# Four graph layers on one core: the gathering engine of three row passes waits for free ring slots once for five groups instead of once for each

## The chip, the cores and the metric

The kernel runs on one core of a Trainium2 chip. Its time is the device time of one execution in microseconds (us). Before the change it is 13066.63 us, the median of three runs (13045.7 to 13079.47).

## The reference

Four graph layers, each after a layer norm and a relu, are added to a node table `x` of 12,500 rows of 128 numbers. A graph of 200,000 edges joins the rows; the edges are sorted by `dst`, and `dst` is denser at low numbers (`12500 * u**2`). What all four layers share is a sum over edges:

```
h = relu(layernorm(x)); x = x + gcn_two_convolutions(h)       # two sums over edges: passes 0 and 1
h = relu(layernorm(x)); neigh = segment_sum(h[src], dst)      # pass 2, which also sums edge_weight
h_NN = sum(h) - neigh;  x = x + normalize(h_NN) @ W.T + b
h = relu(layernorm(x)); x = x + weighted_gcn(h, edge_weight)  # pass 3
h = relu(layernorm(x)); x = x + gated_attention_layer(h, node_vec1, src, dst)   # pass 4, then a pass over stored rows
```

All sums are float32 sums to the reference's tolerance. In passes 0 to 2 each float32 row is held as three bf16 parts whose sum is the float32 value.

## The kernel before

The edges form 1563 tiles of 128 (`NT`), in the order of `dst`. The nodes form 98 windows of 128 (`NW`). An item is one pair of a tile and a window that the tile reaches; a pass works through 1664 items (`NI`), in 104 halves of 16 (`HALF`). For one item TensorE (PE) multiplies a one-hot matrix of the tile's destinations by the tile's gathered source rows and adds the product to the PSUM bank of the window.

A pass in three parts (`pass_in_parts`, passes 0, 1 and 2) is made of these workers:

- GpSimd (POOL) runs `gather_tiles`: one indirect DMA for each tile (line 436) brings 128 source rows of 768 bytes into a ring of 64 slots in SBUF. The ring is 8 groups (`RGROUPS`) of 8 tiles (`GT`), and a pass has 196 groups. From group 8 on, line 433 waits, before each group, until the group that lay in these slots is free: `freed + g - groups + 1` counts.
- SyncE (SP) runs `relay_rows`. For each group g in order it waits until group g + lead has landed and counts that up in `s_landed` (lines 444, 445); then it waits until PE has done the last item that reads group g, and counts `s_free` up by one (lines 455, 456). The lead is 4 (`LEAD`). Every fourth group SP first loads four release counts (line 454).
- ScalarE (ACT) builds the 16 one-hot matrices of a half with 16 activations (line 527) and one wide one (line 534), into two buffers; the wide one waits for PE to be done with the half before the last.
- PE, for each half, loads 16 plan words and 4 gates into registers (line 566), waits for the half's one-hots, and at each block of 8 items for landed rows and open banks (lines 570, 571). Each item is then one matmul (line 576) with register arithmetic for its bank and its slot. In pass 2 an item has a second, small matmul (line 579) with the edge weights; only this second one then signals `s_prod`.
- VectorE (DVE) empties a bank when its window is complete (line 556) and opens it for the window 8 later.

Passes 3 (`pass_with_weights`) and 4 call the same `gather_tiles` and `relay_rows`, with other tables; pass 4 has a ring of 4 groups and a lead of 2. Each pass is one block: none begins before the one before it has ended on all engines.

Of the kernel before, what the change touches and what calls it, by code (L numbers as in the profile page):

```python
# [6 lines left out]
F = 128  # L7
# [2 lines left out]
READY_STEP = 4  # L10
RGROUPS = 8
LEAD = 4
Z_RGROUPS = 4
Z_LEAD = 2
BLOCK = 8
ACC_BANKS = 8
NPARTS = 3
# [33 lines left out]
def gnn_kernel(nc, x, src, dst, edge_weight, node_vec1, L0_W1, L0_b1, L0_W2, L0_b2, L1_W, L1_b, L2_W, L2_b,  # L51
# [17 lines left out]
    TGROUPS = TILES // GT  # L69
# [25 lines left out]
    with ctx:  # L95
# [3 lines left out]
        def sem(name):  # L99
            return ctx.enter_context(nc.semaphore(name))  # L100

        def dram(name, shape, dt=f32):
            return nc.dram_tensor(name, shape, dt, kind="Internal").ap()
# [7 lines left out]
        table16 = dram("table_parts", [NPAD, NPARTS * F], bf16)  # L111
# [22 lines left out]
        ring16 = big[:, 0:RSLOTS * RW].bitcast(bf16).rearrange("p (u f) -> p u f", f=2 * RW)  # L134
# [61 lines left out]
        s_prod = sem("product_done")  # L196
# [135 lines left out]
        def one_window(ap, w):  # L332
            return windows(ap, w).rearrange("p w f -> p (w f)")
# [84 lines left out]
        s_free = sem("rows_free")  # L418

        def tiles_of(g):  # L420
            return min(GT, NT - g * GT)

        def landed_count(no, g):

            whole = sum(tiles_of(k) for k in range(g % RGROUPS, TGROUPS, RGROUPS))
            return 16 * (no * whole + sum(tiles_of(k) for k in range(g % RGROUPS, g + 1, RGROUPS)))

        def gather_tiles(pool, no, tab, slots, groups, width):

            freed = no * (TGROUPS - RGROUPS)  # L430
            for g in range(TGROUPS):
                if g >= groups:
                    pool.wait_ge(s_free, freed + g - groups + 1)
                for k in range(tiles_of(g)):
                    t = g * GT + k
                    pool.indirect_dma_start(  # L436
                        out=slots[:, t % (groups * GT), 0:width], out_offset=None, in_=tab,
                        in_offset=bass.IndirectOffsetOnAxis(ap=idx_tab[:, t // P, t % P:t % P + 1], axis=0),
                    ).then_inc(gathered[g % RGROUPS], 16)

        def relay_rows(sp, no, groups, lead, s_done, done0):

            def landed(g):
                sp.wait_ge(gathered[g % RGROUPS], landed_count(no, g))
                sp.sem_inc(s_landed[no], 1)

            for g in range(lead):
                landed(g)
            for g in range(TGROUPS):
                if g + lead < TGROUPS:  # L450
                    landed(g + lead)
                if g + groups < TGROUPS:
                    if g % 4 == 0:
                        releases = table_values(sp, RELEASE, g, 4, NI)
                    sp.wait_ge(s_done, releases[g % 4] + done0)
                    sp.sem_inc(s_free, 1)

        def table_values(eng, tab, start, n, largest):

            _, vals = nc.values_load_multi_w_load_instructions(  # L460
                tab[:, bass.ds(start, n)], engines=[eng.engine], min_val=0, max_val=largest,
                skip_runtime_bounds_check_because="the tables hold numbers of windows, slots and items")
            return vals
# [26 lines left out]
        def end_values(eng, w):  # L490

            return table_values(eng, bound_tab, w, min(5, NW - w), NI)
# [16 lines left out]
        def pass_in_parts(no, from_acc, sums_of, finish, count_weights=False):  # L509

            items0 = no * NI

            with nc.Block() as block:
                @block.gpsimd
                def _(pool):
                    gather_tiles(pool, no, table16, ring16, RGROUPS, NPARTS * F)

                @block.sync
                def _(sp):
                    relay_rows(sp, no, RGROUPS, LEAD, s_prod, items0)  # L520

                @block.scalar
                def _(act):
                    for q in range(HALVES):
                        for u in range(HALF):
                            col = q * HALF + u
                            last = nc.scalar.activation(apart_flat[:, u * P:(u + 1) * P], iota_col[:], ACT.Abs,  # L527
                                                        bias=dl_tab[:, col:col + 1], scale=-1.0)
                        last.then_inc(s_apart, 1)
                        act.wait_ge(s_apart, no * HALVES + q + 1)  # L530
                        if q >= 2:
                            act.wait_ge(s_prod, items0 + (q - 1) * HALF)
                        half = onehot16_flat[:, q % 2 * HALF * P:(q % 2 + 1) * HALF * P]
                        nc.scalar.activation(half, apart_flat, ACT.Relu, bias=ones[:, 0:1], scale=-1.0).then_inc(s_onehot, 1)  # L534
                        act.wait_ge(s_onehot, no * HALVES + q + 1)

                @block.vector
                def _(dve):
                    def fill(w):
                        b = w % ACC_BANKS  # L540
                        if from_acc:
                            nc.vector.tensor_copy(bank[b][:, 0:F], one_window(acc, w))
                            nc.vector.memset(bank[b][:, F:NPARTS * ACW], 0.0).then_inc(s_open[no], 1)
                        else:
                            nc.vector.memset(bank[b][:, 0:NPARTS * ACW], 0.0).then_inc(s_open[no], 1)

                    dve.wait_ge(s_cleared, no + 1)
                    for w in range(ACC_BANKS):
                        fill(w)
                    for w in range(NW):  # L550
                        if w % 5 == 0:
                            ends = end_values(dve, w)
                        dve.wait_ge(s_prod, ends[w % 5] + items0)
                        sums = sums_of(w)
                        held = psum_parts[:, w % ACC_BANKS, :, 0:sums.shape[-1]].rearrange("p a f -> p f a")
                        nc.vector.tensor_reduce(sums, held, AX.X, ALU.add).then_inc(s_evicted, 1)  # L556
                        dve.wait_ge(s_evicted, no * NW + w + 1)
                        if w + ACC_BANKS < NW:
                            fill(w + ACC_BANKS)
                        finish(dve, w, sums)  # L560

                @block.tensor
                def _(pe):
                    open_banks(s_cleared)
                    for q in range(HALVES):
                        plan, gates = plan_values(pe, q)
                        pe.wait_ge(s_onehot, no * HALVES + q + 1)
                        for u in range(HALF):
                            if u % BLOCK == 0:
                                pe.wait_ge(s_landed[no], gates[2 * (u // BLOCK)])  # L570
                                pe.wait_ge(s_open[no], gates[2 * (u // BLOCK) + 1])
                            b, r = plan[u]
                            m = onehot16[:, q % 2 * HALF + u, :]
                            held = psum_parts[:, bass.ds(b, 1), :, 0:F].rearrange("p o a f -> p (o a) f")
                            rows_t = ring16[:, bass.ds(r, 1), :].rearrange("p o (a f) -> p (o a) f", f=F)
                            last = nc.tensor.matmul(held, m, rows_t, start=False, stop=False, skip_group_check=True)  # L576
                            if count_weights:
                                held = psum_parts[:, bass.ds(b, 1), :, F].rearrange("p o a -> p (o a)")
                                last = nc.tensor.matmul(held, m, ew_parts[:, q * HALF + u, :], start=False, stop=False, skip_group_check=True)  # L579
                            last.then_inc(s_prod, 1)  # L580
# [9 lines left out]
        def pass_with_weights(no):  # L590
# [3 lines left out]
            with nc.Block() as block:  # L594
                @block.gpsimd
                def _(pool):
                    gather_tiles(pool, no, table, ring32, RGROUPS, F)

                @block.sync
                def _(sp):  # L600
                    relay_rows(sp, no, RGROUPS, LEAD, s_prod, items0)

# [886 lines left out]
        no = 4  # L1489
        items0 = no * NI  # L1490
# [10 lines left out]
        with nc.Block() as block:  # L1501
            @block.gpsimd
            def _(pool):
                gather_tiles(pool, no, ptable, ring, Z_RGROUPS, ACW)

            @block.sync
            def _(sp):
                relay_rows(sp, no, Z_RGROUPS, Z_LEAD, s_added, PSLOTS)

# [159 lines left out]
        no = 5  # L1669
        items0 = no * NI  # L1670
# [232 lines left out]
```

## Time and profile before

| | us |
|---|---|
| median of 3 runs | 13066.63 |
| profiled execution | 13160.48 |
| its span, first to last instruction | 13158.7 |
| stretch of pass 0 | 270 to 2560 |
| stretch of pass 1 | 2676 to 4973 |
| stretch of pass 2 | 5029 to 7324 |
| stretch of pass 3 | 7440 to 9699 |
| stretch of pass 4 | 9839 to 12246 |

The page of the profile gives busy time by engine and by line; a matmul's end is modelled. "idle before" is the time in which an engine did nothing ahead of an instruction, and what ended it. "issue" there means that the profile shows nothing that the engine waited for; SPq is SyncE's own queue. A "x" number counts instructions. PEclk is the granted TensorE clock as a share of full speed: 0.50 is the lower level, 1.2 GHz.

### The profile page before, as it was taken

How to read it: one execution, taken by the hardware profiler on the slowest of the kernel's cores; microseconds unless marked ns; L12 is line 12 of the kernel's file. 1: busy time of each engine (PE TensorE's matmuls, PEld its weight loads, DVE VectorE, ACT ScalarE, POOL GpSimd, SP SyncE). 2: the span in 40 equal slices, each digit the busy share in tenths (PEclk: the TensorE clock that was granted, in tenths of full speed). 3: DMA queues.
4: the chain of work that ended last, by engine and by line, in shares of the span. 5: the costliest groups of instructions: out<-in, count | busy, mean ns of one | idle time of the engine just before them, and what ended most of it. 6: DMA issues, size and time to landing. Idle time of an engine off the chain costs nothing. (4 is left out here: it accounts for less than half of the span.)

```text
span 13158.7 us, 95241 instructions
## 1 busy us (share of the span) xinstructions
PE 5061.2 (38%) x19461; PEld 2969.6 (23%) x19461; DVE 3455.4 (26%) x8008; ACT 3221.1 (24%) x7260; POOL 8501.4 (65%) x8989
## 2 busy tenths in 40 slices
PE   1223222432222233333333433433363333333698
PEld 0000000210000001111111322333352223333466
DVE  4000000200000111000000311112235555666887
ACT  3223333323333333223333300000020000101454
POOL 5666666556666664666666566666656666666798
PEclk5555555655555555555555555555575555555888
DMA  3222222222222222222222111111114444444333
GB/s 99 68 69 68 69 68 68 65 77 68 68 70 67 69 68 84 68 68 69 68 69 68 48 46 47 46 46 46 46 56 128 134 134 134 135 137 139 129 135 117
DMA packets 676226, 1070.51 MB, mean 81 GB/s; under 512 B 150819, under 2 KB 518699, under 8 KB 648827
## 3 DMA queue, kind: packets, MB, share of 16 engines
q0 software_dynamic: 329072, 676.05, 19.7%
q10 hardware_dynamic: 247712, 225.10, 5.3%
q1 hardware_dynamic: 98955, 163.50, 3.8%
q8 instruction: 229, 3.75, 0.1%
q14 instruction: 258, 2.11, 0.0%
HBM read 904.63 MB, written 161.05 MB: 81 GB/s over the span
## 5 line engine op out<-in xcount | busy, mean ns | idle before, releaser
L436 POOL DMA_INDIRECT big<-table_parts,tile_cols x4689 | 4460.9, 951 | 2509.2 <-issue 1428.2
L576 PE MATMUL psum<-big 128*128 x4992 | 2099.4, 480 | 4391.0 <-issue 4047.5
L436 POOL DMA_INDIRECT big<-ptable,tile_cols x1563 | 1520.1, 973 | 881.2 <-issue 464.5
L436 POOL DMA_INDIRECT big<-table,tile_cols x1563 | 1486.0, 951 | 751.5 <-issue 463.2
L576 PEld LDWEIGHTS psum<-big 128*128 128x128 bf16 x4992 | 515.4, 103 | 5674.5 <-issue 5674.5
L534 ACT ACTIVATE big<-big,ones 128x2048 bf16<-128x2048 bf16 x312 | 624.6, 2002 | 4707.4 <-PE psum L576 2436.2
L527 ACT ACTIVATE big<-iota_col,dl_tab 128x128 bf16<-128x128 f32 x4992 | 1491.5, 387 | 33.2 <-PEq L694 12.5
L1575 PE MATMUL psum<-acc,big 128*128 x3328 | 882.7, 434 | 1530.4 <-issue 884.3
L644 PE MATMUL psum<-big 128*128 x3328 | 845.4, 394 | 1398.9 <-issue 1353.2
L556 DVE TENSOR_REDUCE acc<-psum 128x128 f32<-128x384 f32 (+1 forms) x196 | 109.7, 560 | 4296.3 <-PE psum L579 1621.1
L1575 PEld LDWEIGHTS psum<-acc,big 128*128 128x128 f32 x3328 | 723.8, 307 | 1689.1 <-issue 1677.1
L644 PEld LDWEIGHTS psum<-big 128*128 128x128 f32 x3328 | 695.6, 283 | 1550.1 <-issue 1544.7
L610 DVE TENSOR_SCALAR big<-iota_col,dl_tab,ew_tab 128x128 f32<-128x128 f32 x1664 | 437.2, 366 | 1816.4 <-PE psum L644 912.4
L1685 POOL TENSOR_SCALAR big<-iota_col,dl_tab,tile_cols 128x128 f32<-128x128 f32 x936 | 748.1, 812 | 119.3 <-POOLq L1613 64.3
L1531 DVE TENSOR_REDUCE wide<-big 128x128 f32<-128x2048 f32 x208 | 772.2, 3712 | 3.3 <-ACT big L1600 3.2
L1553 DVE SCALAR_TENSOR_TENSOR big<-big,sc,psum 128x130 f32<-128x130 f32 x1664 | 509.8, 345 | 969.8 <-remote 650.3
L1780 PE MATMUL psum<-big 128*128 128x129 f32 x3328 | 603.3, 322 | 28.4 <-POOL big L1685 23.8
L556 DVE TENSOR_REDUCE big<-psum 128x128 f32<-128x384 f32 x98 | 54.7, 558 | 2098.1 <-PE psum L576 1597.2
L626 ACT COPY acc<-psum 128x128 f32<-128x128 f32 x98 | 26.1, 267 | 2189.7 <-remote 1089.2
L1780 PEld LDWEIGHTS psum<-big 128*128 128x128 f32 x3328 | 478.6, 215 | 149.8 <-issue 149.3
L1600 ACT ACTIVATE big<-big 128x2048 f32<-128x2048 f32 x104 | 199.7, 1920 | 1200.4 <-DVE wide L1535 844.6
L579 PE MATMUL psum<-big 128*128 128x3 bf16 x1664 | 333.8, 201 | 264.6 <-issue 263.2
(296 smaller groups left out, 4260.2 us busy)
## 6 DMA issues: line engine op xcount, KB each, us to landing
big<-dl_rows ACTq DMA_DIRECT2D x104, 1024.0 KB
zrows<-big ACTq DMA_DIRECT2D x104, 1024.0 KB
big<-zrows SPq DMA_DIRECT2D x104, 1024.0 KB
big<-table_parts,tile_cols POOLq DMA_INDIRECT x4689
table_parts<-big SPq DMA_DIRECT2D x42, 672.0 KB, 3.5
big<-table,tile_cols POOLq DMA_INDIRECT x1563
big<-ptable,tile_cols POOLq DMA_INDIRECT x1563
ptable<-big SPq DMA_DIRECT2D x14, 455.0 KB, 4.0
```

The source lines that it names most:

```text
L436: pool.indirect_dma_start(out=slots[:, t % (groups * GT), 0:width], out_offset=None, in_=tab, in_offset=bass.IndirectOffsetOnAxis(ap=idx_t ...
L527: last = nc.scalar.activation(apart_flat[:, u * P:(u + 1) * P], iota_col[:], ACT.Abs, bias=dl_tab[:, col:col + 1], scale=-1.0)
L534: nc.scalar.activation(half, apart_flat, ACT.Relu, bias=ones[:, 0:1], scale=-1.0).then_inc(s_onehot, 1)
L576: last = nc.tensor.matmul(held, m, rows_t, start=False, stop=False, skip_group_check=True)
L579: last = nc.tensor.matmul(held, m, ew_parts[:, q * HALF + u, :], start=False, stop=False, skip_group_check=True)
L610: last = nc.vector.tensor_scalar(wide_onehot[:, q % 2 * HALF + u, :], iota_col[:], dl_tab[:, col:col + 1], ew_tab[:, col:col + 1], ALU.is_ ...
L644: nc.tensor.matmul(held, wide_onehot[:, q % 2 * HALF + u, :], rows_t, start=False, stop=False, skip_group_check=True).then_inc(s_prod, 1)
L1531: nc.vector.tensor_reduce(part[:, k, :], rows_of, AX.X, ALU.add).then_inc(s_part, 1)
L1553: nc.vector.scalar_tensor_tensor(zbuf[:, h, u, 0:ACW], dyn(ring_flat, slots[u], ACW), in_win[:, h, u:u + 1], bank[n % Z_BANKS][:, 0:ACW], ...
L1575: nc.tensor.matmul(bank[n % Z_BANKS][:, 0:ACW], onehot_t[:, q % 2, u * P:(u + 1) * P], dyn(acc_flat, at[u], ACW), start=True, stop=True).t ...
L1685: return eng.tensor_scalar(onehot[:, q % 2 * HALF + u, :], iota_col[:], dl_tab[:, col:col + 1], weight_tab[:, col:col + 1], ALU.is_equal, ...
L1780: nc.tensor.matmul(dyn(sums_at, at[u], SCW), onehot[:, q % 2 * HALF + u, :], msg[q % MSGS][:, u, 0:SCW], start=False, stop=False, skip_gro ...
```

## The change

```diff
 LEAD = 4
+RUN, RUN_LEAD = 5, 2
...
-        def gather_tiles(pool, no, tab, slots, groups, width):
+        def gather_tiles(pool, no, tab, slots, groups, width, run=1):
 
             freed = no * (TGROUPS - RGROUPS)
             for g in range(TGROUPS):
-                if g >= groups:
-                    pool.wait_ge(s_free, freed + g - groups + 1)
+                if g >= groups and (g - groups) % run == 0:
+                    pool.wait_ge(s_free, freed + min(g - groups + run, TGROUPS - groups))
...
-                    gather_tiles(pool, no, table16, ring16, RGROUPS, NPARTS * F)
+                    gather_tiles(pool, no, table16, ring16, RGROUPS, NPARTS * F, RUN)
...
-                    relay_rows(sp, no, RGROUPS, LEAD, s_prod, items0)
+                    relay_rows(sp, no, RGROUPS, RUN_LEAD, s_prod, items0)
```

In passes 0, 1 and 2 POOL waits only before groups 8, 13, 18 and so on to 193, each time until the slots of the five groups that follow are free (before group 193, of the three that are left). It then issues these groups with no wait between them. SP in these passes looks for landed group g + 2 instead of g + 4 before it goes on to the release of group g; with a lead of 4 the release of the fifth group would wait for a group that POOL has not issued yet. Passes 3 and 4 stay as they are.

## Rows read from the trace of the kernel before

**Rows 1.** The page: its span.
```profile
span 13158.7 us, 95241 instructions
```

**Rows 2.** The page's costliest groups: line, engine, operation, count | busy, mean | idle before.
```profile
L436 POOL DMA_INDIRECT big<-table_parts,tile_cols x4689 | 4460.9, 951 | 2509.2 <-issue 1428.2
L576 PE MATMUL psum<-big 128*128 x4992 | 2099.4, 480 | 4391.0 <-issue 4047.5
```

**Rows 3.** Busy time by stretch: passes 0, 1, 2 (start:end, length, engines, clock, DMA).
```profile
270.00:2560.00 2290.00, 672.42 (x1680) 176.32 (x1680) 127.56 (x390) 705.32 (x1768) 1487.03 (x1563) 0.54 0.25 67
2676.00:4973.00 2297.00, 672.69 (x1680) 176.24 (x1680) 174.44 (x585) 705.37 (x1768) 1485.14 (x1563) 0.53 0.25 67
5029.00:7324.00 2295.00, 876.30 (x3344) 351.08 (x3344) 110.92 (x293) 705.40 (x1768) 1488.70 (x1563) 0.50 0.25 67
```

**Rows 4.** Waits of POOL in passes 0, 1, 2: us in total, times, longest.
```profile
POOL big L436 <- SPq L456: 293.0, 46, 11.8
POOL big L436 <- SPq L456: 299.8, 47, 11.7
POOL big L436 <- SPq L456: 296.3, 72, 12.7
```

**Rows 5.** Waits of PE in pass 1, the longest in total.
```profile
PE psum L576 <- issue: 1495.5, 708, 7.2
```

**Rows 6.** Timeline of PE in pass 1: start, busy, line, count, idle before.
```profile
3663.89 0.48 PE L576 MATMUL psum<-big 128*128 x1 [2.32 <-issue]
...
3668.86 2.90 PE L576 MATMUL psum<-big 128*128 x8 [1.63 <-issue]
3673.90 4.52 PE L576 MATMUL psum<-big 128*128 x13 [2.13 <-ACT big L534]
3679.73 0.48 PE L576 MATMUL psum<-big 128*128 x1 [1.31 <-issue]
```

**Rows 7.** Timeline of POOL over the same pause.
```profile
3661.77 0.95 POOL L436 DMA_INDIRECT big<-table_parts,tile_cols  x1 [0.30 <-issue]
3669.67 0.95 POOL L436 DMA_INDIRECT big<-table_parts,tile_cols  x1 [6.95 <-SPq L456]
```

**Rows 8.** Stretches of pass 1; columns PE, PEld, DVE, ACT, POOL.
```profile
3612.70:3622.70 10.00, 5.54 (x17) 1.71 (x17) 0.00 (x0) 9.29 (x20) 7.56 (x9) 0.67 0.25 69
3622.70:3627.70 5.00, 3.36 (x10) 0.94 (x9) 1.79 (x6) 4.27 (x15) 3.99 (x4) 0.50 0.29 79
3627.70:3662.70 35.00, 5.73 (x12) 1.25 (x12) 1.05 (x4) 6.78 (x17) 26.55 (x28) 0.50 0.30 79
...
2676.80:2756.80 80.00, 26.46 (x46) 7.70 (x44) 3.52 (x16) 24.49 (x66) 60.73 (x64) 0.50 0.29 78
2756.80:2806.90 50.10, 7.66 (x16) 1.66 (x16) 0.00 (x0) 6.78 (x17) 37.93 (x40) 0.50 0.29 79
...
4938.50:4972.70 34.20, 23.14 (x68) 6.95 (x68) 9.70 (x28) 15.57 (x35) 0.08 (x1) 0.65 0.01 4
```

**Rows 9.** Stretches of pass 2, two PE instructions to an item, the same columns.
```profile
6127.10:6137.10 10.00, 6.57 (x29) 2.80 (x27) 0.93 (x3) 9.90 (x23) 7.59 (x8) 0.50 0.25 70
6137.10:6142.10 5.00, 0.81 (x3) 0.31 (x3) 0.00 (x0) 3.31 (x12) 3.80 (x4) 0.50 0.30 80
6142.10:6156.90 14.80, 2.59 (x8) 0.83 (x8) 1.13 (x3) 0.00 (x0) 11.37 (x12) 0.50 0.29 80
6156.90:6161.60 4.70, 1.31 (x4) 0.41 (x4) 0.00 (x0) 0.15 (x1) 0.05 (x2) 0.50 0.07 22
5029.70:5109.70 80.00, 25.65 (x57) 8.92 (x55) 3.06 (x8) 17.77 (x49) 60.71 (x64) 0.50 0.29 78
5109.70:5129.80 20.10, 2.74 (x9) 0.93 (x9) 0.00 (x0) 6.78 (x17) 15.16 (x16) 0.50 0.30 79
5129.80:5142.50 12.70, 2.68 (x9) 0.92 (x9) 0.00 (x0) 0.00 (x0) 0.03 (x1) 0.50 0.03 8
7286.80:7323.60 36.80, 29.40 (x128) 13.21 (x127) 5.12 (x12) 13.33 (x34) 0.05 (x1) 0.50 0.02 4
```

## The prediction

> **What bounds the kernel now.** I read the span [rows 1], then the costliest groups [rows 2]: the gathers of the three changed passes keep POOL busy for 4461 us, more than any other group, with 2509 us idle before them; PE's matmuls of these passes have 4391 us of idle before them, nearly all put down to "issue". The table by pass [rows 3] shows three passes of the same length, 2290 to 2297 us, each with all 1563 gathers. A gather comes every 1.25 us when nothing holds POOL (0.95 busy and 0.30 idle [rows 7]; 64 of them fill 80 us [rows 9]). So a pass has a floor of 1563 x 1.254 = 1960 us of issuing. On top come POOL's waits for SP's release at line 456: 293, 300 and 296 us [rows 4]. Only these 889 us, and what follows the last gather, can the change move. Passes 3 and 4 keep their code.
>
> The release comes from PE, so the next view is PE's. It works at two speeds. While POOL issues, a matmul of pass 1 comes every 2.80 us (0.48 busy, 2.32 idle), and the profile names nothing that it waits for (1495 us of such idle in pass 1 [rows 5]); then 8 come in 2.90 us and 13 in 4.52 us [rows 6]. The clock does not make this: both stand at 0.50 in most of these stretches [rows 8]. What does turn it is POOL. POOL's last gather before the pause begins at 3661.77 and ends at 3662.7 [rows 7]; PE turns fast at 3668.86, 6.1 us later, POOL resumes at 3669.67, and PE is slow again from about 3678.4, 8.7 us after that [rows 6]. I call the first lag the turn and the second the carry. PE is thus slow during most of POOL's issuing, POOL (one tile in 1.25 us) outruns it, fills the ring and stops; PE then recovers. POOL and PE limit each other, and every pause costs a turn, in which both are slow or idle, and brings a carry, in which both work.
>
> **The change part by part.** Satisfied waits cost nothing: the rhythm is the same 1.25 us across a group's start as within a group [rows 8, 9], so dropping 150 of 188 waits per pass saves nothing by itself; what they cost when unsatisfied is in the 889 us. SP's lead of 2: SP has only the release chain on its queue; PE sees rows up to two groups past the one it works in, and its gate looks 8 items, about one group, ahead. I take zero. Upper bound: one gather's interval on each of the 38 releases, 48 us per pass, if SP's steps came that late. Lower bound: SP no longer holds a release back for group g + 4, but that group has landed long before in a full ring, so no gain either.
>
> What remains is the length of the pauses. There are now 46, 47 and 72 of them [rows 4]; there will be 38 per pass (groups 8, 13, ... 193), each until five groups are free. At the resume three groups (24 tiles) lie in the ring, where now there are seven.
>
> Demand: 1664 items in 1563 tiles, so five groups want 42.6 items.
>
> Passes 0 and 1. In the 50.1 us of issuing five groups PE did 17 + 10 items in 15 us and 12 in the other 35 [rows 8]; a stretch late in a long run gives 16 in 50.1, 0.32 per us. For the first 15 us I take 24, three fewer than this row, since the ring then holds only 24 tiles and PE's gate works in blocks of 8; then 35 x 0.34 = 12: 36 items. 6.6 are left at the pause. In the turn of 6.1 us PE does 2, the other 4.6 go at 21 items in 9.6 us, 2.2 per us [rows 6], in 2.1 us: a pause of 8.2 us. The nearest row, 6.95 us after 40 tiles [rows 7], is the lower bound; the upper is 9.3 (only 20 items in the first 15 us, since the ring holds just 24 tiles). The first wait stands at 80 us, not at 130: PE has done 46 less 16 clearing matmuls, 30 items [rows 8], 10 short of the 40 that five dense groups want. A turn after so long a run I put at 10 us (between 6.1 after 40 tiles and more than 11.7 after 104 [rows 4, 8]), then 7 items in 3 us: 13 us. Sum: 13 + 37 x 8.2 = 316, against 293 and 300: +23 and +16. After the last wait POOL issues three groups (19 tiles, 24 us) instead of one, and PE works beside them: PE ends some 22 us after the last gather instead of 34 [rows 8], -12 in pass 1; for pass 0, whose end I did not lay out, I take a third of that, -4. Together +23 us.
>
> Pass 2. An item is two matmuls here, so PE does fewer items beside the gathers: (57 - 16) / 2 = 20 items in the first 80 us, 4.5 in the next 20.1, 0.22 per us; at the end of a run of 24 tiles 8 / 2 = 4 in 14.8 us, 0.27 per us [rows 9]. The carry gives (29 + 3) / 2 = 16 items in the first 15 us. In 50 us: 16 + 35 x 0.25 = 25 items; 17.6 are left. The fast rate is that of the end, 64 items in 36.8 us, 1.74 per us. The turn is about 4 us after 24 tiles and over 10 after 80 (POOL stood still for 12.7 us with only 9 matmuls in them [rows 9]); for 40 tiles 6.4, with 1.6 items. 16 / 1.74 = 9.2: a pause of 15.6. The same working for 24 tiles gives 6.8 us where the mean is 296.3 / 1563 x 24 = 4.6 [rows 4], so it is 2.2 too dear per cycle. I take 13.5, between 15.6 and the 10.5 that scaling by that ratio gives. First wait: 20 items done, 20 to go, 10 + 10 = 20 us. Sum: 20 + 37 x 13.5 = 520 against 296, +223; the end -5. Together +218 us.
>
> So the mechanism in one line: fewer pauses mean fewer carries (72 to 38 in pass 2), and the carries are where PE kept up at no cost; the saved turns do not make up for it.
>
> Sum: +23 + 218 = +241 us, 13160.5 to about 13400 for the profiled execution. The profiled execution stands 94 us above the median; I carry the difference over unchanged: 13067 + 241 = 13308.
>
> A rule that speaks against it: the Trainium skill, page "Runtime: NRT & Kernel Launch", section "Instruction fetch mechanics", says that an engine's instructions are streamed ahead and that the dispatch rate hides this. By it PE's stream would not be slow beside POOL's gathers; at the fast rate [rows 6] PE would do 42.6 items in 19 us of the 50, POOL would never wait, and the change would be worth zero. The 165 waits [rows 4] say that something in the stream is slow, whatever it is; the profile does not name it.
>
> **The rivals.** *No change.* The pause grows in proportion to the tiles issued: 300 us for 1563 tiles is 7.7 us per 40, and POOL already issues runs of 40 with 6.95 us behind them [rows 7, 8]. For it: passes 0 and 2 differ much in the number of their waits and hardly in their sum [rows 4], which no fixed cost per pause explains. Against: in pass 2 the items left after a longer run are more. 13,067 plus or minus 39. The page's rule above would also end here.
>
> *Faster.* In a longer pause the gathers' effect on PE drains fully, and the carry after it lasts 15 us instead of 8. Pass 2 then does 12 more items in the carry, its pause falls by 7 to 6.5 us, 20 + 240 - 296 - 5 = -41; in passes 0 and 1 the pause falls to 7 and the first to 11, -23 and -30, and the ends -4 and -12. In all -110 us: 12,957. It decides from a carry of about 12 us on. For it: the carry after a pause much longer than the turn is in no row here. Against: the pause of 6.95 us gave 8.7 [rows 6, 7].
>
> *PE runs out of rows.* 24 tiles lie in the ring, the next 8 land 12 us after the resume. If the carry is a span of time and not a number of instructions, what PE misses in it is lost: 6 items at 0.45 us in passes 0 and 1, 2.7 x 74 = +200 on top, 13,510. Against: 24 tiles are 25 items, and PE does about 17 to 20 in the carry.
>
> **How the numbers follow.** Main case 0.55, no change 0.15, faster 0.17, out of rows 0.13. The main case's own range: pauses of 7.2 and 10.5 us give +56; 9.3 and 15.6 give +404: 13,120 to 13,470. The whole range reaches down into no change and up to the last rival: 13,040 to 13,500. A measurement of this kernel tells 0.3%, 39 us, from no change. Slower by more: 0.55 + 0.13 and some of the no-change case's edge, 0.70; same 0.13; faster 0.17.
>
> **What would show it.** POOL's waits for line 456: 38 in each changed pass, mean near 8.2 us in passes 0 and 1 and 13.5 in pass 2, with pass 2 the one that grows most; passes 3 and 4 unchanged. PE: after POOL's stop slow for 6 us or more, fast until about 8 to 9 us after the resume. PE's idle put down to SP's line 445 should stay near nothing; if it doesn't, PE ran out of rows. Wrong: waits in pass 2 of 8 us or less, a carry of 12 us or more, or a change in passes 3 and 4.

## The result and the profile after

The changed kernel takes 13474.26 us (median of 4 runs, 13460.44 to 13489.95); the kernel before, run beside it, 13062.94 us. The ratio is 1.0315, 95% interval 1.0298 to 1.0333: 411 us slower. The forecast was 241 us slower.

The profiled execution took 13489.95 us, only 16 us above its median, where that of before stood 98 us above. Between the two profiles lie 329.5 us, and the views below account for those. First the stretches of passes 0 to 4 in the changed kernel, from the first gather to PE's last item (start:end, length, then busy time and counts of PE, PEld, DVE, ACT, POOL, then the granted clock, the busy share of the DMA engines and GB/s). The changed kernel has one line more ahead of the gathers, so lines 445, 456 and 576 of before are 446, 457 and 577 here.

```profile
274.00:2652.00 2378.00, 666.02 (x1680) 175.96 (x1678) 128.21 (x392) 704.59 (x1767) 1484.96 (x1563) 0.53 0.24 65
2768.00:5124.00 2356.00, 665.42 (x1680) 176.03 (x1678) 174.97 (x586) 704.45 (x1767) 1484.65 (x1563) 0.54 0.24 66
5180.00:7712.00 2532.00, 868.45 (x3344) 351.16 (x3343) 111.26 (x294) 704.75 (x1767) 1484.90 (x1563) 0.50 0.23 61
7827.00:10071.00 2244.00, 843.64 (x3344) 687.69 (x3344) 438.00 (x1664) 51.79 (x196) 1489.61 (x1563) 0.58 0.18 46
10206.00:12583.00 2377.00, 886.67 (x3328) 724.31 (x3328) 1433.30 (x2699) 232.44 (x309) 1519.21 (x1563) 0.57 0.46 136
```

Against [rows 3] passes 0, 1 and 2 are longer by 88, 59 and 237 us, with nearly the same counts and busy time: 384 us in the three, where the forecast has 241. Passes 3 and 4 (2259 and 2407 us before) are shorter by 15 and 30; their code is the same. POOL's waits in passes 0, 1 and 2 (total, times, longest), which answer to [rows 4]:

```profile
POOL big L437 <- SPq L457: 391.8, 30, 24.1
POOL big L437 <- SPq L457: 369.2, 34, 23.8
POOL big L437 <- SPq L457: 548.4, 38, 21.2
```

They grew by 99, 69 and 252 us, fewer and longer: in pass 2 72 waits of 4.1 us became 38 of 14.4. One cycle of pass 2, at two PE instructions to an item: the first 10 us after a resume, the next 5, the other 35.2 us of issuing, and the pause:

```profile
5852.20:5862.20 10.00, 7.54 (x34) 3.33 (x32) 0.00 (x0) 6.86 (x18) 7.57 (x8) 0.50 0.27 70
5862.20:5867.20 5.00, 1.14 (x6) 0.41 (x4) 0.00 (x0) 1.00 (x4) 3.80 (x4) 0.50 0.31 82
5867.20:5902.40 35.20, 5.50 (x17) 1.76 (x17) 1.13 (x3) 0.00 (x0) 26.85 (x28) 0.50 0.29 78
5902.40:5914.30 11.90, 6.73 (x28) 2.81 (x27) 0.00 (x0) 5.89 (x15) 0.00 (x0) 0.50 0.04 10
```

17 items, 3, then 8.5 in 35 us (0.24 per us), and 14 in the pause. The prediction had 16 in the first 15 us, then 0.25 per us. Over the 36 runs of 40 gathers between two pauses of pass 2, PE starts 18.3 items in the first 15 us (15 to 22), 8.3 in the next 35 and 15.4 in the pause, so the carry is somewhat larger than forecast and the rate after it is as forecast. Pass 1 has something else as well. Two runs of 40 tiles that follow each other, and the pause after the second:

```profile
3044.30:3094.50 50.20, 14.65 (x39) 3.89 (x38) 0.00 (x0) 17.03 (x46) 37.87 (x40) 0.57 0.29 77
3094.90:3145.10 50.20, 7.64 (x16) 1.67 (x16) 0.00 (x0) 6.78 (x17) 37.97 (x40) 0.50 0.29 77
3145.10:3168.40 23.30, 9.63 (x26) 2.67 (x26) 1.79 (x6) 10.27 (x24) 0.00 (x0) 0.57 0.02 5
```

POOL's timeline between and after them:

```profile
3093.10 0.95 POOL L437 DMA_INDIRECT big<-table_parts,tile_cols  x1 [0.30 <-issue]
3094.93 0.95 POOL L437 DMA_INDIRECT big<-table_parts,tile_cols  x1 [0.88 <-issue]
...
3168.54 0.95 POOL L437 DMA_INDIRECT big<-table_parts,tile_cols  x1 [23.74 <-SPq L457]
```

At 3093 five groups were as good as free when POOL came for them, so it paused for 0.9 us only. The run that followed had no carry: 16 items beside 40 gathers where the run before it had 39. All the catching up fell into a pause of 23.7 us. This is no single case. In passes 0 and 1, eleven runs of 40 gathers begin after a pause of less than 5.7 us; PE starts 4 to 12 items in their first 15 us, where it starts 19 to 29 after a longer pause, and the pause behind them is 16 to 24 us long. Six more pauses of 22 to 24 us follow 80 gathers with no real pause between them.

PE did not run out of rows. Its idle time put down to SP's landed count (line 446) is one row in pass 0, one in pass 2 and none in pass 1:

```profile
PE psum L577 <- SPq L446: 7.3, 1, 7.3
...
PE psum L577 <- SPq L446: 3.8, 2, 2.3
```

### The profile page after: what moved, and what is told of

The parts are those of the page before. It is cut to its first block and busy times, and to the rows that moved or that the text cites. A ratio compares the mean times of both kernels' runs of the same rounds, so it can differ in the third digit from the quotient of the medians.

```text
span 13488.2 us, 95241 instructions
## 1 busy us (share of the span) xinstructions
PE 5020.1 (37%) x19461; PEld 2952.4 (22%) x19461; DVE 3454.6 (26%) x8008; ACT 3219.9 (24%) x7260; POOL 8494.6 (63%) x8989
## 5 line engine op out<-in xcount | busy, mean ns | idle before, releaser
L577 PE MATMUL psum<-big 128*128 x4992 | 2081.8, 478 | 4736.2 <-issue 4387.4
L645 PE MATMUL psum<-big 128*128 x3328 | 829.9, 383 | 1400.2 <-issue 1326.4
```

What stands on the lines that cost most here:

```text
L645: nc.tensor.matmul(held, wide_onehot[:, q % 2 * HALF + u, :], rows_t, start=False, stop=False, skip_group_check=True).then_inc(s_prod, 1)
```

## The experiments

Two questions: which part of the change costs, and why PE is slow beside the gathers at all. I call PE held back where it is slow in this way. The runs fell on five chips, and the kernel before took 13,136, 11,452, 11,458, 11,458, 13,174 and 11,453 us in the six groups of runs. That difference became the main finding; each run is read against the kernel before on its own chip. The chip that came twice took 11,458 and 11,453 us. Where an edit adds lines, the line numbers in the views are higher; the texts name what stands there.

**The lead alone.** `RUN, RUN_LEAD = 1, 2`.

> Only SP's lead is changed (2 instead of 4); POOL waits at every group, as before. Theory (carries: PE is slow beside POOL's gathers, and what a pause gives is a carry of some 8 us in which PE is still fast; fewer pauses, fewer carries): no change, 13,063 within 0.3%, about 47, 47 and 72 waits of POOL. Rival (the lead: SP shows rows to PE too late): a good part of the 411 us is here, over 13,150, and PE's idle put down to SP's landed count grows from 1 us to tens of us.

Ratio 1.0003 (0.999 to 1.0015) on the 13,136 us chip. The lead costs nothing. PE's waits for line 446 sum to 0.6 us in pass 1 and 6.2 us in pass 2. POOL waits 49, 52 and 78 times, for 295, 308 and 306 us, about as before.

**Three groups at a time.** `RUN, RUN_LEAD = 3, 4`.

> POOL waits for three groups at a time, SP's lead is 4 as before. Theory (carries): before the change pass 2 already issued 24 tiles between pauses, and passes 0 and 1 32 to 40, so 63 waits per pass take away few pauses: 13,070 to 13,150, pauses in pass 2 of about 5 us after 24 tiles. Rival (PE runs out of rows after a pause, since the ring holds 40 tiles and not 56): idle of PE put down to SP's landed count, and a time that grows in proportion to the groups waited for, about half of the 411 us: 13,250.

Ratio 1.0179 (1.0162 to 1.0196), 13,360 us, far outside the 13,070 to 13,150 expected. The rival named about the right total for a reason that the trace denies: hardly any wait of PE for rows (2.7 us, in pass 2). POOL's waits in the three passes:

```profile
POOL big L437 <- SPq L457: 373.2, 31, 18.2
POOL big L437 <- SPq L457: 386.8, 31, 17.9
POOL big L437 <- SPq L457: 367.9, 63, 11.6
```

and two neighbouring waits of pass 1 on POOL's timeline:

```profile
3156.97 0.95 POOL L437 DMA_INDIRECT big<-table_parts,tile_cols  x1 [11.19 <-SPq L457]
...
3226.89 0.94 POOL L437 DMA_INDIRECT big<-table_parts,tile_cols  x1 [10.19 <-SPq L457]
```

They end 69.9 us apart: 48 tiles of 1.25 us and one pause. At every other wait three groups were already free and POOL went on, so passes 0 and 1 fell into runs of six groups. I had counted on their natural 32 to 40 tiles, but a wait for r groups only lets POOL stop at multiples of r. In pass 2 the runs stayed at 24 tiles, and the pauses became 5.8 us in the mean where [rows 4] give 4.1: a pause for three groups also ends later than one for the next group.

**Five groups in pass 2 alone.** Both changed arguments get `if no == 2`, the old value otherwise.

> Waits for five groups, with the lead of 2, in pass 2 alone; passes 0 and 1 are those of before. Theory (carries): pass 2 lost the most pauses (72 to 40), so it holds most of the loss: +220 to +260 us, 13,300; passes 0 and 1 hold the rest, 150 us. Rival (the cost is that of a wait for five groups, wherever it stands): a third of 411, 13,200.

Ratio 1.0206 (1.0189 to 1.0223), +271 us. Passes 0 to 2:

```profile
POOL big L437 <- SPq L457: 301.8, 51, 11.9
POOL big L437 <- SPq L457: 310.4, 52, 12.0
POOL big L437 <- SPq L457: 580.7, 38, 21.3
```

Passes 0 and 1 wait as before [rows 4], and two thirds of the whole loss are in pass 2: the theory's side, a little above its 220 to 260 us.

**Without the second matmul.** The changed kernel without the edge-weight sums: `pass_in_parts(2, ..., add_bias(1))` with no `count_weights=True`.

> The changed kernel without the second matmul of each item in pass 2: the sums of the edge weights are left out. Theory (PE beside the gathers does one instruction of any kind in 0.70 us, so the second matmul with its two address instructions costs 2.1 us per item there): pass 2 becomes like passes 0 and 1, items 2.8 us apart beside the gathers, POOL's waits 9 to 11 us in the mean instead of 14; from POOL's first gather to PE's last item 2340 to 2380 us instead of 2530; the kernel 13,290 to 13,330. Rival (the pauses of pass 2 come from the five groups alone, PE's second matmul hides under the first as it does in the fast stretches, 0.13 us per item): pass 2 stays over 2480 us, 13,430 or more.

Ratio 1.0157 (1.014 to 1.0174) to the kernel before, where the changed kernel has 1.0315: about 208 us back. Pass 2 took 2362 us instead of 2532, as long as passes 0 and 1 beside it (2363 and 2358). POOL's waits in it:

```profile
POOL big L437 <- SPq L457: 378.3, 34, 22.9
```

and PE's timeline beside the gathers in it (start, length, idle before it):

```profile
5409.84 0.48 PE L577 MATMUL psum<-big 128*128 x1 [2.32 <-issue]
5412.64 0.48 PE L577 MATMUL psum<-big 128*128 x1 [2.32 <-issue]
5415.44 0.48 PE L577 MATMUL psum<-big 128*128 x1 [2.32 <-issue]
```

Items come 2.80 us apart as in [rows 6], where pass 2 with both matmuls had some 4.2 us in the mean (0.24 items per us above). So what is slow beside the gathers is PE's instruction stream, not the matmul: fewer instructions to an item, a shorter item. I had expected 2.1 us for the second matmul; it is 1.4.

The trace also records PE's register instructions, which no view prints: one or two work out bank and slot ahead of each matmul. In the fast stretches of pass 1 they take 0.14 and 0.04 us. While PE is held back they take 0.70 us. In pass 1 of the kernel before, 1106 of 3328 are 0.6 us or longer.

**Spaced gathers.** The kernel before, with POOL memsets behind each gather of passes 0 to 2 (the edit is shortened: `reps` is 1 or 2, and the text in angle brackets stands for the column):

```
                    ).then_inc(gathered[g % RGROUPS], 16)
+                    for _ in range(reps if no < 3 else 0):
+                        if spaced[0] >= 2:
+                            pool.wait_ge(s_pad, 4 + spaced[0] - 1)
+                        nc.gpsimd.memset(<one of two scratch columns>, 0.0).then_inc(s_pad, 1)
+                        spaced[0] += 1
```

> The kernel before, with one tiny GpSimd memset (128x1) behind each gather in passes 0 to 2, so that gathers come some 1.40 us apart instead of 1.25. Theory (a backlog: the gathers' work comes a little faster than something that PE's stream shares with them can clear it; the turn of 6.2 us after 50 us of issuing says some 12% faster): at 1.40 us the backlog hardly builds, PE stays fast for most of the time, POOL's waits fall from 300 us to under 60 per pass, and a pass takes 1563 x 1.40 = 2190 us and some 25: faster than before by up to 70 us per pass, 12,850 to 13,050. Rival (PE is slow beside any gather in work, whatever the spacing): PE goes at 2.80 us per item beside the gathers as before, issuing takes 230 us more per pass with 76 items more done beside it, worth 30 us of pause; POOL's waits fall to 220 us or so: +150 us per pass, 13,500.

> Two such memsets behind each gather, some 1.55 us between gathers. Theory (backlog): POOL's waits near zero, PE fast throughout (the idle of PE is then waiting for landed rows), a pass is 1563 x 1.55 = 2420 us: slower than before by 130 us per pass, 13,450. Rival (slow beside any gather): waits of POOL of 150 us and more in each of the passes remain, 13,900.

Ratios 1.001 (0.9999 to 1.0021) and 0.9997 (0.9987 to 1.0007). Neither expectation could be tested. The memsets ran in the gap and left the interval as it was; POOL's timeline with two of them:

```profile
2999.26 0.95 POOL L438 DMA_INDIRECT big<-table_parts,tile_cols  x1 [0.16 <-issue]
3000.21 0.14 POOL L446 MEMSET spacer<- 128x1 f32 x2
3000.51 0.95 POOL L438 DMA_INDIRECT big<-table_parts,tile_cols  x1 [0.16 <-issue]
```

And the kernel before itself took 11,452 us on this chip, where PE is not held back. What memsets in the gap do where it is held back was not run. The control for the run without weight sums, on the same chip, shows what is different.

> The control for the run without weight sums: the kernel before, with the second matmul of pass 2 left out as there. Theory (carries): pass 2 becomes like pass 1 of the kernel before, runs of 32 to 40 tiles, 47 waits of POOL and not 72, and since short pauses had made up for the second matmul, hardly faster: 2285 to 2300 us from first gather to last item, where it was 2293. Rival (the second matmul costs POOL's waits in the kernel before too): 2200 us or less.

11,452.65 us (one run, the second matmul of pass 2 left out). Its three passes:

```profile
266.00:2229.00 1963.00, 589.47 (x1679) 177.36 (x1678) 127.46 (x390) 704.57 (x1767) 1482.21 (x1563) 0.54 0.29 79
2347.00:4308.00 1961.00, 589.70 (x1677) 177.44 (x1677) 174.09 (x584) 705.02 (x1768) 1480.66 (x1563) 0.54 0.29 79
4367.00:6335.00 1968.00, 589.91 (x1677) 177.13 (x1676) 110.49 (x292) 704.69 (x1768) 1487.83 (x1563) 0.55 0.29 78
```

and PE's timeline beside the gathers in pass 1 (line 445 is SP's landed count):

```profile
3000.22 2.75 PE L576 MATMUL psum<-big 128*128 x8 [7.24 <-SPq L445]
3010.26 2.88 PE L576 MATMUL psum<-big 128*128 x8 [7.29 <-SPq L445]
```

PE does each block of 8 in 2.75 us with POOL issuing all the while, and then waits 7 us for the next rows. POOL never waits for the ring: a pass is its 1960 us of issuing. The clock is not the difference: 0.54 in pass 1 here against 0.53 [rows 3]. As a control for the other kind of chip the run says nothing, so what the second matmul costs in the kernel before there was not measured.

**The changed kernel on a chip of that kind.**

> The changed kernel once more, beside the kernel before on the same chip. One chip ran the kernel before in 11,452 us: there PE's matmuls come 8 in 2.75 us beside the gathers and POOL never waits for the ring. Theory (the change's cost is that of longer pauses, and these exist only where PE is slow beside the gathers): if this chip is like that one, no wait of POOL for the release and a ratio of 1.000 within 0.2%; if the kernel before takes some 13,100 here, a ratio of 1.03 again. Rival (waiting for five groups has a price of its own, say POOL reaching group 13 before five are free): a ratio over 1.005 on a chip of either kind, with waits of POOL in the trace.

11,451.52 us against 11,458.39, ratio 0.9999 (0.999 to 1.0007), and no row of POOL waiting for line 457. This settles the cost: on a chip where PE is not held back the change costs nothing, because the waits are satisfied whether they are asked for one group or five. Of PE's 11,648 register instructions in passes 0 to 2, none is longer than 0.18 us.

**A wider interval.** Three memsets of 128x64 behind each gather, on three chips; only the third holds PE back.

> The kernel before with three GpSimd memsets of 128x64 behind each gather in passes 0 to 2; one and two memsets of 128x1 fitted into the 0.30 us between gathers and left the interval at 1.25 us, these should make it 1.40 to 1.55. On a chip where PE is slow beside the gathers: theory (a backlog that 12% more room would clear) says PE fast nearly throughout, POOL's waits under 60 us per pass, passes of 2190 to 2420 us set by the interval alone; rival (slow beside any gather): PE stays at 2.80 us per item in pass 1, POOL still waits 150 us and more per pass on top. On a chip where PE is never slow both say the same: each pass longer by 1563 times the added interval, 230 to 470 us, 12,150 to 12,850 in all.

> The kernel with three memsets behind each gather of passes 0 to 2 (1.475 us between gathers) once more, in search of a chip on which the kernel before takes some 13,100 us. There: theory (a backlog that builds because gathers come some 12% too fast, and does not build at 1.475 us) says passes 0 to 2 at the length set by the interval, 2330 us each, nearly no waits of POOL, 13,200; rival (PE slow beside any gather) says waits of POOL of 150 us and more per pass on top, 2450 to 2550 us in passes 0 and 1 and more in pass 2, 13,700 or more. On a chip where the kernel before takes 11,450 this tells nothing new: 12,580.

> The same kernel as in the two runs before (1.475 us between gathers in passes 0 to 2), for the same question, on whatever chip comes. Where the kernel before takes some 13,100 us: theory (a backlog that 18% more room clears) 13,200 with passes 0 to 2 at 2330 us and hardly a wait of POOL; rival (PE slow beside any gather) 13,700 or more, with 150 us and more of waits per pass on top. Where it takes 11,450: 12,570, and the question stays open.

POOL's timeline on the third chip:

```profile
3000.03 0.95 POOL L437 DMA_INDIRECT big<-table_parts,tile_cols  x1
3000.98 0.38 POOL L445 MEMSET wide<- 128x64 f32 x3
3001.51 0.95 POOL L437 DMA_INDIRECT big<-table_parts,tile_cols  x1
```

The interval is 1.48 us. On the chips where the kernel before takes 11,458 us the ratios are 1.0984 (1.0964 to 1.1003) and 1.096 (1.0912 to 1.1008): passes 0 to 2 longer by some 368 us each, within the 230 to 470 expected. On the last chip the kernel before takes 13,173.79 us and this one 13,305.37, ratio 1.0101 (1.0071 to 1.013). Its passes 0 to 4:

```profile
275.00:2615.00 2340.00, 590.73 (x1680) 177.70 (x1679) 127.54 (x390) 704.70 (x1768) 2081.28 (x6252) 0.54 0.25 66
2734.00:5075.00 2341.00, 591.35 (x1680) 178.03 (x1680) 174.20 (x584) 705.02 (x1768) 2081.38 (x6252) 0.54 0.25 66
5133.00:7479.00 2346.00, 779.41 (x3343) 350.55 (x3342) 110.50 (x292) 704.63 (x1767) 2086.55 (x6252) 0.50 0.25 66
7596.00:9857.00 2261.00, 874.03 (x3344) 702.32 (x3343) 436.16 (x1663) 51.49 (x196) 1487.46 (x1563) 0.57 0.18 46
9993.00:12394.00 2401.00, 884.36 (x3328) 725.47 (x3328) 1433.33 (x2697) 232.48 (x309) 1518.67 (x1563) 0.57 0.46 134
```

PE's timeline in pass 1, where [rows 6] showed single matmuls 2.80 us apart (line 452 is SP's landed count here):

```profile
3010.47 2.81 PE L583 MATMUL psum<-big 128*128 x8 [10.00 <-SPq L452]
3022.36 2.76 PE L583 MATMUL psum<-big 128*128 x8 [9.08 <-SPq L452]
```

PE is fast beside gathers 1.48 us apart. Passes 0 to 2 have no wait of POOL for the release left, and passes 3 and 4, whose gathers still come every 1.25 us, take what they took before; POOL's waits in pass 3 for the release (line 463 here; 285.8 us in 62 waits in the kernel before) are

```profile
POOL big L437 <- SPq L463: 289.5, 64, 12.9
```

In this one execution no register instruction of PE is longer than 0.18 us in passes 0 to 2, and 549 of 3328 are 0.6 us or longer in pass 3. The theory had said 13,200 and 2330 us per pass, the rival 13,700 or more; the run gave 13,305 and 2340 to 2346. So PE is not slow beside every gather. Each of these passes is 44 to 51 us longer than in [rows 3], though the issuing alone grew by some 350. One rival is left: the memsets differ from plain gathers in more than the interval, and no run put memsets into the gap, with the interval kept, on a chip that holds PE back.

The traces of such chips tell how a hold ends. From the start of a run of gathers to the end of PE's last register instruction of 0.6 us or more it takes 33 us after 24 gathers (three groups at a time, pass 2), 55 after 40 (the changed kernel), 67 after 48 (three groups at a time) and 112 after 80 (the changed kernel, pass 0), each the median: 1.38 to 1.40 us for each gather. Where a pause is shorter than that takes, the rest is carried over: from 3044.3 on, above, 80 gathers with the pause of 0.9 us between them hold PE for 110.7 us. That is what a backlog cleared at 1.40 us per gather would do, and it is why a pause of 0.9 us brings no carry.

**Just below the limit.** Three memsets of 128x40, in passes 0 to 3.

> The kernel before with three memsets of 128x40 behind each gather in passes 0 to 3, for an interval of about 1.42 us instead of 1.25. The turns of the kernel before say that what is shared clears one gather in 1.40 us: PE turns fast 34.4 us after the start of a run of 24 tiles and 112.7 us after one of 80, 78.3 us for 56 more tiles. Theory (backlog): on a chip where the kernel before takes some 13,150 us, gathers 1.42 us apart leave no backlog, POOL's waits of passes 0 to 3 are near zero, each of these passes takes 1563 x 1.42 = 2220 us and some 6 instead of 2290 (2257 for pass 3), and the kernel is faster than both by 200 to 250 us: 12,930. Rival (the limit lies between 1.42 and the 1.475 that was seen to be free of it): PE is slow at times, pauses return on top of the longer interval, 13,150 to 13,400. Where the kernel before takes 11,450 there is nothing to gain: 4 x 260 us more, 12,480.

12,710.67 us against 11,453.0, ratio 1.1099 (1.1073 to 1.1126). It fell on a chip that does not hold PE back. The gathers come 1.43 us apart and pass 0 takes 2267 us from the first gather to PE's last item. Whether a smaller spacing beats both kernels on the other kind of chip stays open; no version in these runs did.

## Why the prediction was right, and where its sizes were off

Right: the direction; that satisfied waits cost nothing; that the lead costs nothing (the lead alone, 1.0003); that PE does not run out of rows; that fewer pauses mean fewer carries and longer pauses, most of all in pass 2. The first waits of the passes were put at 13, 13 and 20 us and are 13.3, 13.0 and 21.2. Pass 2's 38 waits were put at 520 us and measured 548. That closeness is partly a choice: the working gave 15.6 us for a pause and the scaling 10.5, and 13.5 was taken between them; the mean is 14.4.

The mis-sized terms:

- The pause of 8.2 us in passes 0 and 1 (38 waits, 316 us per pass): measured 30 waits of 13.1 us and 34 of 10.9, 392 and 369 us. The cycle was worked out as one that repeats. It does not where five groups are free almost as POOL comes for them: a pause shorter than the turn brings no carry, and the debt is paid in the next pause, 16 to 24 us long. After pauses of 6 to 12 us the next one has 7.0 us in pass 0 and 8.7 in pass 1, so the 8.2 holds for the plain cycle, and the 76 + 53 = 129 us that were missed belong to the uneven ones. In pass 2 28 us were missed. I had the uneven cycles in no case.
- The upper bound of 9.3 us for that pause. With the 20 items that it names, the same sum gives 10.0 us, and the top of the range some 13,520 instead of 13,470.
- The ends. The prediction had PE end 22 us after the last gather in pass 1; it was some 34, so the 12 us counted back were not there.
- Passes 3 and 4 came out 45 us shorter with unchanged code, and hide part of this in the profile. The prediction named a change there as a sign of being wrong, and it stays unexplained: from first to last gather these passes take 2221 and 2348 us, where the other profiles on chips of this kind (the kernel before and five experiments) have 2231 to 2237 and 2367 to 2381.
- The conversion to the median. The difference of profile and median was carried over unchanged, 94 us. It was 98 before and 16 after, so of the 411 us 82 are not in the two profiles.

The rivals: "no change" fell on chips that hold PE back and holds on the other kind, there because no wait is unsatisfied. "Faster" fell: it needed a carry of 12 more items after a long pause. In pass 2 the first 15 us hold 17.0 items after pauses of 12 to 14 us and 19.4 after 14 to 18, and in the cycle above PE was down to 3 items in 5 us already 10 us after the resume. "PE runs out of rows" fell by the rows of line 446.

The prediction took a page's rule to say that PE's stream can't be slow; that goes further than the page. The Trainium skill's "Runtime: NRT & Kernel Launch", section "Instruction fetch mechanics", has the fetch of an engine's instructions hidden behind the rate at which they are dispatched. The runs give both kinds of stream: on three chips PE's is never behind (8 items in 2.75 us beside the gathers), and on the others it is, beside gathers 1.25 us apart and not beside gathers 1.48 apart. No run tried whether fetching is what suffers. The DMA records of the traces speak against it: the first of the two instruction queues moved

```profile
q8 instruction: 229, 3.75, 0.1%
```

(packets, MB, share of the DMA engines' time) on both kinds of chip, at 1.07 us for a packet in the kernel before and in the changed kernel on the 11,458 us chip. So the rule may hold on both, and the slow step lie elsewhere.

Shown: the cost needs a held-back PE (none on the other kind of chip), most of it lies in the pass with more PE instructions to an item and leaves when these are taken out, and gathers spaced by memsets remove the hold. Argued only: that the thing shared is a queue which clears a gather in 1.40 us. The ends of the holds and the spaced run fit it; the step at which the hold sets in was seen only to lie between 1.25 and 1.48 us. Open: what is shared, and why some chips hold PE back and others do not, or whether it is the chip at all and not something else that stayed the same with it.

## What to carry to other kernels

Where two engines limit each other through a ring, how often the leading one pauses can matter more than how long: ask what the pause gives the other engine afterwards, and do not make waits coarser because most of them are satisfied. If an engine's idle time ends in "issue" with a steady period while another engine issues DMAs, spacing the DMAs is a test that tells whether they are the reason; here it took the hold away and still made no kernel faster (1% slower where PE is held back, 10% where it is not). And run the kernel before beside every experiment: the same program took 11,452 us on one chip and 13,174 on another.

## What the runs showed of the hardware

- The same kernel differs by 14 to 15% between chips (11,452 to 11,458 us on three, 13,063 to 13,174 on the others), with the same granted clock (0.575 and 0.579), the same 1.25 us between gathers and the same busy times of ACT. The difference lies in the passes with gathers: pass 1 of the kernel before takes 2297 us, and 1961 on the other kind of chip.
- Held back, PE's register instructions take 0.70 us each instead of 0.14 and 0.04: 3245 of 11,648 in passes 0 to 2 of the kernel before are 0.6 us or longer, none on the other kind of chip. Items of pass 1 are then 2.80 us apart [rows 6], those of pass 2 4.2 in the mean, and the second matmul removed brings pass 2 to 2.80.
- In pass 4, which is slower too (2407 us, some 2010 on the other kind of chip), no register instruction is that long; what is slow there was not looked into.
- A hold ends 1.38 to 1.40 us for each gather after the run of gathers began (33, 55, 67 and 112 us for 24, 40, 48 and 80).
- Two GpSimd memsets of 128x1 fit behind a gather without moving the next (1.25 us); three of 128x40 move it to 1.43, three of 128x64 to 1.48.
